# Attention and conv block: one of three buffers an image, and where the projection's bias is added

## The reference

```python
x = x + window_attention(_gn(x))      # 7x7 windows, shifted by 3, 8 heads; ends in x @ proj_weight.T + proj_bias
x = x + conv3x3(_gn(x))               # 128 -> 128 channels, SAME, weights made from sign and clip
# _gn: group norm, 32 groups of 4 channels, mean and variance over all pixels of an image
```

## Time and profile before

| | before |
|---|---|
| time, median of 3 runs | 3631.72 us (3628.21 to 3633.22) |
| the profiled execution | 3628.35 us, its span 3626.5 us |
| mean granted clock of PE | 0.995 |
| PE busy | 3415.0 us, 94% of the span |
| DVE busy | 3045.9 us, 84% |
| ACT busy | 2630.5 us, 73% |
| POOL busy | 2322.2 us, 64% |
| line 555, x_a to x_b | 128 instructions |
| line 761, x_b to x_c | 160 instructions |

### The profile page before, as it was taken

How to read it: one execution, slowest core, us unless ns; L and a number is a source line. 1 busy time by engine, 2 the same in 40 slices (tenths; PEclk the granted TensorE clock), 3 DMA queues, 4 the chain that set the end, 5 groups by cost and what they waited for, 6 DMA issues and landing times.

```text
span 3626.5 us, 141183 instructions
## 1 busy us (share of the span) xinstructions
PE 3415.0 (94%) x57227; PEld 2799.3 (77%) x57227; DVE 3045.9 (84%) x7552; ACT 2630.5 (73%) x5857; POOL 2322.2 (64%) x3674
## 2 busy tenths in 40 slices
PE   2999999999999999999999999999999999999997
PEld 1778778778778778778777778777778778788785
DVE  5788888888888888888888888888888888888885
ACT  1777777777777777777777777777777777777772
POOL 4476666766666766666766666766667766657763
PEclk9999999999999999999999999999999999999998
DMA  2011101111101111101111111111111111111001
GB/s 57 20 30 33 33 25 30 36 33 36 33 25 30 36 33 36 33 23 33 35 34 35 28 28 33 33 35 36 28 28 33 33 36 33 30 25 33 18 18 29
DMA packets 213331, 113.75 MB, mean 31 GB/s; under 512 B 8784, under 2 KB 212688, under 8 KB 212688
## 3 DMA queue, kind: packets, MB, share of 16 engines
q1 hardware_dynamic: 212688, 104.72, 11.0%
HBM read 53.31 MB, written 51.38 MB: 29 GB/s over the span
## 4 chain that ended last, share of the span: by engine, by line
PE 51%; DVE 23%; POOL 12%; issue 11%; ACT 2%; SPq 0%; DVEq 0%; POOLq 0%; DMA 0%; ACTq 0%
PE conv_ps L994 14%; PE qkv_ps L875 10%; PE attn_ps L913 7%; PE probsT_ps L899 7%; PE scores_ps L888 5%; DVE s_sb L743 4%; POOL s_sb L404 3%; DVE plane_lo L755 3%; PE misc_ps L875 2%; DVE s_max L748 2%; DVE x_b L791 2%; PE misc_ps L961 2%; PE misc_ps L957 2%; PE misc_ps L951 2%; POOL x_n L444 1%
## 5 line engine op out<-in xcount | busy, mean ns | idle before, releaser
L404 POOL TENSOR_TENSOR s_sb<-s_sb,s_max 113x392 f32<-113x392 f32 x1024 | 1027.7, 1004 | 1127.6 <-DVE s_max L748 1123.2
L899 PE MATMUL probsT_ps<-ident,probs 113*128 113x113 f32 x4096 | 586.4, 265 | 72.6 <-ACT probsT L466 72.5
L460 ACT ACTIVATE probs<-s_sb 113x392 f32<-113x392 f32 x1024 | 551.6, 539 | 128.3 <-POOL s_sb L404 124.8
L432 POOL TENSOR_TENSOR plane<-x_n 128x224 f32<-128x224 f32 x896 | 601.3, 692 | 18.7
L913 PEld LDWEIGHTS attn_ps<-v,probsT 128*49 128x49 f32 x16384 | 465.4, 125 | 181.9 <-issue 160.3
L748 DVE TENSOR_REDUCE s_max<-s_sb 113x8 f32<-113x392 f32 x1024 | 574.6, 561 | 35.3
L527 ACT COPY v<-qkv_ps 64x256 f32<-64x256 f32 (+2 forms) x1280 | 393.6, 327 | 287.7 <-PE qkv_ps L875 281.6
L466 ACT COPY probsT<-probsT_ps 128x392 f32<-128x392 f32 x1024 | 489.5, 478 | 144.6 <-PE probsT_ps L899 140.4
L743 DVE TENSOR_TENSOR s_sb<-scores_ps,bias 113x392 f32<-113x392 f32 x1024 | 564.7, 551 | 8.1 <-PE scores_ps L888 8.1
L913 PE MATMUL attn_ps<-v,probsT 128*49 128x34 f32 x16384 | 566.5, 214 | 3.5 <-DVE o_sb L719 0.6
L899 PEld LDWEIGHTS probsT_ps<-ident,probs 113*128 113x128 f32 x4096 | 431.4, 141 | 129.3 <-ACT probs L460 86.0
(11 more groups left out here) (142 smaller groups left out, 6706.9 us busy)
## 6 DMA issues: line engine op xcount, KB each, us to landing
x_in<-in_x_dram SPq DMA_DIRECT2D x224, 224.0 KB, 2.8
out_dram<-x_out SPq DMA_DIRECT2D x224, 224.0 KB, 2.5
x_b<-in_L_conv_w_dram SPq DMA_DIRECT2D x1, 576.0 KB
x_b<-L_conv_pruning_mask_dram SPq DMA_DIRECT2D x1, 576.0 KB
x_n<-_conv_rel_pos_table_dram SPq DMA_DIRECT2D x14, 10.7 KB
x_n<-in_mask_dram SPq DMA_DIRECT2D x1, 196.0 KB
w_in<-n_L_conv_qkv_weight_dram SPq DMA_DIRECT2D x1, 192.0 KB
ident<-in_ident_dram SPq DMA_DIRECT2D x1, 64.0 KB
```

The lines of the kernel that those rows point to most:

```text
L404: nc.gpsimd.tensor_tensor(s, s, top, ALU.subtract).then_inc(sub_ready, 1)
L432: last = nc.gpsimd.tensor_tensor(plane[:, t % 2, j], *sums[j])
L460: nc.scalar.activation(probs[0:QP, slot % 2, :, :, 0:N], s_sb[0:QP, slot % 4], ACT.Exp)\
L899: last = nc.tensor.transpose(probsT_ps[:, w * 128:w * 128 + QP], probs[0:QP, u % 2, w].rearrange("p e m -> p (e m)"), ident[0:QP, 0:QP])
```

## The change

There are three equal buffers `x_of[0]` to `x_of[2]`, and image n uses `x_of[n % 3]` from its input to its output. The projection is added in place, so both sets of copies (lines 555 and 761) and their two semaphores are gone. What took the copies' place in the order:

- ACT's input tile waits for the conv output of the image that had the buffer before (`conv_out`, two images back), and DVE's first projection tile waits until norm 1 is applied.
- The buffer never holds the projection's bias. Norm 2 adds it to the mean of each channel (one 128x1 add on DVE behind the aggregation, with a semaphore `mv_raw` for it; the variance doesn't change), and its shift becomes (bias - mean) x scale instead of 0 - mean x scale: two POOL instructions as before. Norm 1 has zero in that place.
- The residual misses the bias too. It is put into `m_1`, which enters both row kinds once: ACT evicts it with a bias of `out_bias / wc_scale`, made once at the start by two DVE instructions.

The scratch space for the conv's weights moves to `x_of[1]` and `x_of[2]`.

```diff
-XC_AT = {2: (1, 3), 3: (3, 5), 4: (5, 6), 6: (0, 1), 8: (6, 7)}
-XB_AT = {3: (1, 3), 4: (3, 6), 6: (0, 1), 12: (6, 7)}
...
-        x_a = sb("x_a", [128, H, W])
-        x_b = sb("x_b", [128, H, W])
-        x_c = sb("x_c", [128, H, W])
+        x_of = [sb(f"x_{n}", [128, H, W]) for n in range(3)]
...
+        gn1.kept_out, gn2.kept_out = zero, out_bias
...
-                then(tt(gn.shift[:], gn.mean[:], gn.y[:], ALU.mult))
-                tt(gn.shift[:], zero[:], gn.shift[:], ALU.subtract).then_inc(gn.ready, 1)
+                then(tt(gn.shift[:], gn.kept_out[:], gn.mean[:], ALU.subtract))
+                tt(gn.shift[:], gn.shift[:], gn.y[:], ALU.mult).then_inc(gn.ready, 1)
...
-                                pool.wait_ge(xc_ready, i * len(XC_AT))
...
-                        need(act, xa_free, (i + 1) * len(XB_AT) - (t < TILES - 1))
-                        need(act, gn1.applied, (i + 1) * ROWS)
-                        nc.scalar.copy(flat(x_a)[:, t * TP:(t + 1) * TP].rearrange("c (s p) -> c s p", s=SUB),
+                        need(act, conv_out, (i - 2) * TILES + t + 1)
+                        nc.scalar.copy(flat(x_of[(i + 1) % 3])[:, t * TP:(t + 1) * TP].rearrange("c (s p) -> c s p", s=SUB),
...
-                            nc.scalar.copy(m_1[:], conv_ps[:, 1, 0:PP]).then_inc(m1_ready, 1)
+                            if number == 0:
+                                act.wait_ge(scaled_bias_ready, 1)
+                            nc.scalar.activation(m_1[:], conv_ps[:, 1, 0:PP], ACT.Identity, bias=scaled_bias[:])\
+                                .then_inc(m1_ready, 1)
...
-                    if u in XB_AT and live(i):
-
-                        t0, t1 = XB_AT[u]
-                        copied = [tiles[1] for tiles in XC_AT.values()].index(t1) + 1
-                        need(act, xc_ready, (i - 1) * len(XC_AT) + copied)
-                        need(act, gn2.stat, i * (ROWS + 1) - (2 if 0 < t0 and t1 < TILES else 0))
-                        nc.scalar.activation(flat(x_b)[:, t0 * TP:t1 * TP], flat(x_a)[:, t0 * TP:t1 * TP],
-                                             ACT.Identity, bias=out_bias[:]).then_inc(xa_free, 1)
...
-                vec.bn_aggr(gn.mv[:], gn.stats[:].rearrange("p a b -> p (a b)")).then_inc(gn.mv_ready, 1)
+                vec.bn_aggr(gn.mv[:], gn.stats[:].rearrange("p a b -> p (a b)"))\
+                    .then_inc(gn.mv_raw if gn is gn2 else gn.mv_ready, 1)
+                if gn is gn2:
+                    dve.wait_ge(gn2.mv_raw, img + 1)
+                    vec.tensor_tensor(gn2.mv[:, 0:1], gn2.mv[:, 0:1], out_bias[:], ALU.add).then_inc(gn2.mv_ready, 1)
...
-                    if u in XC_AT and live(i, -1):
-
-                        t0, t1 = XC_AT[u]
-                        need(dve, conv_out, (i - 2) * TILES + t1)
-                        vec.tensor_copy(flat(x_c)[:, t0 * TP:t1 * TP], flat(x_b)[:, t0 * TP:t1 * TP]).then_inc(xc_ready, 1)
...
+                            img = i if u >= PROJ_AT else i - 1
+                            x_img = x_of[img % 3]
                             if t == 0:
-                                dve.wait_ge(xa_free, (i + 1) * len(XB_AT) - 1)
-                            if t == ROWS - 2:
-                                dve.wait_ge(xa_free, i * len(XB_AT))
+                                dve.wait_ge(gn1.applied, (img + 1) * ROWS)
...
-                                at = x_b[:, y0:y0 + n, x0:x0 + m]
+                                at = x_img[:, y0:y0 + n, x0:x0 + m]
...
-                            dve.wait_ge(xc_ready, (img + 1) * len(XC_AT))
...
-                                                     scalar=wc_scale[:], in1=flat(x_c)[:, t * TP:(t + 1) * TP],
+                                                     scalar=wc_scale[:], in1=flat(x_of[img % 3])[:, t * TP:(t + 1) * TP],
...
                 step(vec.tensor_copy(wc_scale[:], conv_ps[:, 0, 0:1]))
+                step(vec.reciprocal(scaled_bias[:], wc_scale[:]))
+                step(vec.tensor_tensor(scaled_bias[:], scaled_bias[:], out_bias[:], ALU.mult))
+                dve.sem_inc(scaled_bias_ready, 1)
```

More of the change, by code:

```diff
@@ L188, in build_block @@
         out_bias = sb("out_bias", [128, 1])
+        scaled_bias = sb("scaled_bias", [128, 1])
         bias = sb("bias", [128, 2, PAIRS, WP, 2, N])
@@ L238, in __init__ @@
                 self.stat = sem(f"{name}_stat")
+                self.mv_raw = sem(f"{name}_mv_raw")
                 self.mv_ready = sem(f"{name}_mv_ready")
@@ L273, in build_block @@
         oT_hi_ready = sem("oT_hi_ready")
-        xa_free = sem("xa_free")
-        xc_ready = sem("xc_ready")
+        scaled_bias_ready = sem("scaled_bias_ready")
         tok_hi_ready, tok_lo_ready = sem("tok_hi_ready"), sem("tok_lo_ready")
@@ L290, in flat @@
             return t[:].rearrange("p a b -> p (a b)")
[L292 to L296, removed]
+        wc_raw = flat(x_of[1])[:, 0:TAPS * C].rearrange("p (t c) -> p t c", c=C)
+        wc_mask = flat(x_of[1])[:, TAPS * C:2 * TAPS * C].rearrange("p (t c) -> p t c", c=C)
+        wc_k = flat(x_of[2])[:, 0:TAPS * C].rearrange("p (t c) -> p t c", c=C)
+        wc_clip = flat(x_of[2])[:, TAPS * C:2 * TAPS * C].rearrange("p (t c) -> p t c", c=C)
+        wc_u = flat(x_of[1])[:, 0:PLANES * KW * C].rearrange("p (t c) -> p t c", c=C)
         wc_sum = flat(x_n)[:, 0:C]
@@ L299, in build_block @@
         wc_absmax = flat(x_n)[:, 2 * C:3 * C]
-        wc_chmax = flat(x_c)[:, 2 * TAPS * C:(2 * TAPS + 1) * C]
+        wc_chmax = flat(x_of[2])[:, 2 * TAPS * C:(2 * TAPS + 1) * C]
         wc_inv = flat(x_n)[:, 4 * C:5 * C]
@@ L420, in body @@
                             y0, y1 = t * TILE_ROWS + (t > 0), min((t + 1) * TILE_ROWS + 1, H)
-                            nc.gpsimd.tensor_scalar(x_n[:, 1 + y0:1 + y1, :], x_c[:, y0:y1, :], gn2.y[:], gn2.shift[:],
+                            nc.gpsimd.tensor_scalar(x_n[:, 1 + y0:1 + y1, :], x_of[(i - 1) % 3][:, y0:y1, :], gn2.y[:], gn2.shift[:],
                                                     ALU.mult, ALU.add).then_inc(gn2.applied, 1)
@@ L443, in body @@
                             rows = slice(1 + row * WIN + rows.start, 1 + row * WIN + rows.stop)
-                            last = nc.gpsimd.tensor_scalar(x_n[:, rows, cols], x_a[:, y0:y0 + n, x0:x0 + m],
+                            last = nc.gpsimd.tensor_scalar(x_n[:, rows, cols], x_of[(i + 1) % 3][:, y0:y0 + n, x0:x0 + m],
                                                            gn1.y[:], gn1.shift[:], ALU.mult, ALU.add)
@@ L773, in body @@
                             dve.wait_ge(misc_free, misc_number(i, kind, t) + 1)
-                            vec.bn_stats(gn1.stats[:, t, :], flat(x_a)[:, t * TP:(t + 1) * TP]).then_inc(gn1.stat, 1)
+                            vec.bn_stats(gn1.stats[:, t, :], flat(x_of[(i + 1) % 3])[:, t * TP:(t + 1) * TP]).then_inc(gn1.stat, 1)
                             if t == TILES - 1:
@@ L796, in body @@
                             for n, (y0, height) in enumerate(spans):
-                                vec.bn_stats(gn2.stats[:, t + n, :], flat(x_b)[:, y0 * W:(y0 + height) * W])\
+                                vec.bn_stats(gn2.stats[:, t + n, :], flat(x_img)[:, y0 * W:(y0 + height) * W])\
                                     .then_inc(gn2.stat, 1)
```

## The result

The changed kernel took 3638.94 us, the median of 16 runs, beside 3630.74 for 16 runs of the kernel before: a ratio of 1.0022, with a 95% interval of 1.0015 to 1.0029. It is some 8 us slower, where 7 us less was forecast, and it lies above the range. One run of each kernel, of 7243.76 us before and 4547.91 after, is in these medians and not in the ratio; without them the medians are 3630.16 and 3638.92, 8.8 apart. The execution that was profiled took 3642.03 us, with a span of 3640.2.

What follows compares the result with a forecast made beforehand. PE was taken to bound the kernel except on two detours per image through DVE and POOL. 31 x (0.30 + 0.08 - 0.19) = 5.9, with 0.4 and 0.7, made 7.0 us less: 3624.7 us, range 3617 to 3634.

Steps and rivals of the forecast that it cites:

- The copy of unit 6: DVE's x_c copy on norm 2's detour: said to be on the chain, so removing it saves 0.30 us an image.
- POOL's 0.08: POOL's subtraction of unit 8, beside a DVE copy: 0.92 us was to become 0.84, saving 0.08 of the chain.
- The add: 128x1 DVE add behind norm 2's aggregation: said to delay the unit's scores by 0.19 us, bounds 0.07 to 0.49.
- The rule on the semaphore: Trainium skill's statement that a semaphore behind each Vector instruction costs nothing extra; it would put the add at 0.07 us.
- So the bias is worth nothing: Bias on ACT's m_1, seven an image: 0.14 us longer each, but said not to delay PE.
- rival 3: Biased m_1 gets on PE's path: one place gives 3629.1 us (chance 0.05), four give 3642.4 (0.05 for four or more).
- the argument on PE's waits: PE waits for ACT only at probsT, ending the two detours, with no m_1 on ACT between POOL's subtraction and the eviction.
- start and tail: First image without conv work and last part without attention: said to save 0.4 and 0.7 us, once each.
- the copies of units 2 to 4 and ACT's four: DVE copies before 1499.54 and ACT's biased copies, 3.8 us an image: said to be covered, worth nothing in the steady part.
- the second: Rival: the add eats the copy's gain; at 0.35 us it gives 3629.8, at 0.49 it gives 3634.3; chance 0.15.
- new wait: ACT's input tile for the conv output, projection's first tile for norm 1: said not to wait; either appearing would refute the prediction.
- PE's wait for probsT: Twice an image, 1.2 us at most, ending the two detours; its growth would show the prediction wrong.

## Why the prediction was wrong

**The step that failed** is "The copy of unit 6 is on the chain: it starts at 1502.71, the instruction behind it at 1503.01, so 0.30 us go." The instruction behind it did start 0.30 earlier, but gn_dev, three further on, takes 0.22 longer, so only POOL's 0.08 is left of it. The rows for it were there: gn_dev's end and that of POOL's subtraction lie 0.02 apart. The prediction noticed that gn_dev took 0.32 beside POOL and 0.16 without, and used that only to price the add. The profile's chain names the copy too:

```profile
1502.71 0.16 DVE x_c L761
...
1503.49 0.33 DVE gn_dev L679
```

It is followed back over semaphores and over the order on each engine. No semaphore stands between gn_dev and POOL, so it counts the time in which gn_dev is held as DVE's own work. The prediction's list of PE's waits also leaves out the one for gn_var, 14.3 us, which is where the end of gn_dev reaches PE.

The Trainium skill (SBUF — State Buffer, section "SBUF: two separate sides") has the rule: the port pair that VectorE and GpSimd share is an exclusive lock; a Vector instruction with two SBUF inputs and a GpSimd instruction that reads SBUF take it whole, whoever starts first, and the other waits. The rows agree in both directions: gn_dev held to POOL's end with two inputs and free at 0.21 with one, and tok_lo at 0.56 or 1.06 by whether it starts 0.08 ahead of x_n or 0.03 behind. Where tok_lo is first, it is POOL that waits: the first of the two x_n takes 1.02 there and 0.67 after.

**POOL's 0.08** was right in size and counted once; it also goes in unit 6, where it holds gn_dev. Together that is the 0.15 of the kernel with neither addition.

**The add** was put at 0.19, from 0.07 to 0.49. The scores start 0.51 behind the aggregation's start, as forecast, 0.20 more than before; they also take 0.57 instead of 0.50, so 0.26 passes to PE. The rule on the semaphore that the prediction weighed would have made it 0.07; the rows decide against it here.

**"So the bias is worth nothing"** failed too. An m_1 takes 0.44 (mean of 224), 0.10 over the copy, less than the 0.14 taken. The one of unit 26 is on the path, as the first part of rival 3 says, with a chance of 0.05, and costs 0.17 rather than 0.14: 0.09 through the eviction, which the argument on PE's waits ruled out because none was named there, and 0.08 through tok_lo. PE did not wait beforehand because the eviction came just in time: the transposes of unit 25 start 0.16 behind its end before and 0.14 after. A cover without slack doesn't appear among the waits.

**The sum** with what was measured: -0.15 + 0.26 + 0.17 = +0.28 an image, within 0.02 of the period's 0.30. 31 x 0.30 = 9.3 us, against 8.2 to 8.8 between the medians; start and tail were to give back 1.1, which these two executions can't show, as the half clock falls differently in their last bodies (98.2 after, 95.9 before). What the copies of units 2 to 4 and ACT's four were worth was right: there ACT runs up to 1.3 us earlier, DVE and POOL up to 0.8, and PE not at all.

**Of the rivals**, the second came nearest: the add ate what the removal gave, and more, because there was only 0.15 to eat. No new wait appeared for the conv output or for norm 1, and PE's wait for probsT grew, which the prediction had named as a sign against it:

```profile
PE probsT_ps L891 <- ACT probsT L463: 62.0, 51, 1.3
DVE m_sum L759 <- ACT m L502: 51.2, 25, 2.1
...
PE conv_ps L986 <- DVE plane_lo L750: 16.1, 26, 0.6
```

These are the waits after the earlier trace rows. PE's wait for probsT rose from 59.1 to 62.0, and that for plane_lo is as it was.

## What to carry to other kernels

Before an instruction is priced at its own length, look at where the next ones on its engine end: if one of them ends within two hundredths of an instruction of another engine in every image, that engine may set the time, and what is removed ahead of it may already be paid for. A tiny Vector instruction that takes two to four times its usual time beside POOL is such a place: giving gn_dev and gn_var one tensor and scalars was worth 0.22 an image here, and removing all nine copies 0.15. A constant was cheapest where it rode on an operation under another engine's work: the same bias cost 0.43 an image at two places, and 0.11 in the eviction of the input.

## What the runs showed of the hardware

Who went first was settled by a lead of 0.02 to 0.08 us, so a delay of 0.10 on ACT became 0.5 on DVE. A 128x1 operand had a price of its own here: on ACT, a bias makes the eviction of 224 elements 441 ns instead of 340 and that of 448 elements 639 instead of 536. By the Trainium skill (ScalarE: Activation LUTs, section "What ACT_TABLE_LOAD costs") each such operand adds about 93 ns; 101 and 103 were measured here against a copy. On DVE, m_sum goes from 381 to 440 with a scalar.

What stays open is the clock. From body 2 to body 30, bodies of over 1.2 us beyond the median all have their half clock at one place, in PE's work after unit 24: one in the changed kernel, three with plain m_1, two without the add, two with neither, one in the kernel before with biased m_1, and none in the kernel before or in the five others. In the rows of body 15 the clock is at half behind a stretch in which PE idled for 0.52 of 2 us. In the four kernels whose gn_dev has one input PE's wait there is 0.83 to 0.88 us and no such body occurs. In the five kernels that have one it is 1.11 to 1.14, but in the kernel before and the one without the copy it is 1.11 and 1.14, and none occurs either. The wait alone does not decide it, and no run here tells what does.
